# Low-rank tile products of a step in one session, down behind them, and a last step without turns on TensorE

## The reference, cut to what matters

```python
x = x + L0_ffn(L0_cond(x, ..., itok_B_2_6))     # x: (128, 32, 512)
x = x + L1_ffn(L1_cond(x, A, B, itok_B_4_50))

def lora_add(base, inp, A, B):                  # rank 16, matrices picked for each of 128 batches
    t = einsum('bri,bni->bnr', A[ids], inp)
    return base + einsum('bor,bnr->bno', B[ids], t) * 0.5
# L0_cond
gate = lora_add(x @ W_gate.T, x, A_gate, B_gate)            # 512 -> 1376
up   = lora_add(x @ W_up.T,   x, A_up,   B_up)
act  = silu(gate) * up
down = lora_add(act @ W_down.T, act, A_down, B_down)        # 1376 -> 512
# L0_ffn: down @ sign(weight).T + bias
# L1_cond: rank-16 pair picked for each batch (no base product); L1_ffn: linear with 8 adapters, + bias
```

## Time and profile before

| | us |
|---|---|
| median of 3 runs (924.7 to 925.49) | 925.48 |
| the profiled execution | 923.36 |
| its span | 921.4 |
| TensorE busy | 913.8 (99%) |
| DVE busy | 440.0 (48%) |
| ACT busy | 196.0 (21%) |
| POOL busy | 93.4 (10%) |
| granted TensorE clock, mean | 1.00 |

### The profile page before, as it was taken

How to read it: one execution, slowest core, us unless ns; L and a number is a source line. 1 busy time by engine, 2 the same in 40 slices (tenths; PEclk the granted TensorE clock), 3 DMA queues, 4 the chain that set the end, 5 groups by cost and what they waited for, 6 DMA issues and landing times.

```text
span 921.4 us, 27817 instructions
## 1 busy us (share of the span) xinstructions
PE 913.8 (99%) x10528; PEld 709.0 (77%) x10528; DVE 440.0 (48%) x1051; ACT 196.0 (21%) x350; POOL 93.4 (10%) x81
## 2 busy tenths in 40 slices
PE   9999999999999999999999999999999999999998
PEld 6887777778787777777877778787777777877775
DVE  5753435544444454454445544443454454444534
ACT  6742111111212112112111111212112112111111
POOL 0210001111010111101011111010111101011111
PEclk9999999999999999999999999999999999999999
DMA  9934445555454455555445555454455545445541
GB/s 345 414 106 130 120 121 140 141 155 147 134 143 123 132 141 147 155 138 145 130 122 138 141 155 146 134 142 126 127 144 148 153 134 149 124 128 139 141 118 53
DMA packets 148247, 135.22 MB, mean 147 GB/s; under 512 B 53633, under 2 KB 119937, under 8 KB 148097
## 3 DMA queue, kind: packets, MB, share of 16 engines
q1 hardware_dynamic: 90576, 108.16, 40.6%
q10 hardware_dynamic: 56704, 23.62, 10.1%
q0 software_dynamic: 944, 3.15, 0.9%
HBM read 92.11 MB, written 11.01 MB: 112 GB/s over the span
## 4 chain that ended last, share of the span: by engine, by line
PE 99%; DMA 0%; issue 0%; DVE 0%; ACT 0%; SPq 0%
PE gu_ps L790 54%; PE y_ps L834 28%; PE gu_ps L923 4%; PE out_ps L854 3%; PE out_ps L891 3%; PE y_ps L790 1%; PE out_ps L843 1%; PE out_ps L790 1%; PE gu_ps L914 1%; PE out_ps L864 1%; DMA lb_raw<-in_lbw 0%; PE gu_ps L963 0%; PE gu_ps L1035 0%; PE y_ps L895 0%; PE gu_ps L970 0%
## 5 line engine op out<-in xcount | busy, mean ns | idle before, releaser
L834 PE MATMUL y_ps<-down_sb,actT_sb 128*128 128x512 f32 x1056 | 258.9, 398 | 0.0
L790 PE MATMUL gu_ps<-wg_sb,xT_sb 128*128 128x512 f32 (+1 forms) x1152 | 256.0, 371 | 0.0
L790 PE MATMUL gu_ps<-wu_sb,xT_sb 128*128 128x512 f32 (+1 forms) x1152 | 251.4, 367 | 0.0
L790 PEld LDWEIGHTS gu_ps<-wg_sb,xT_sb 128*128 128x128 f32 x1152 | 204.4, 188 | 55.2 <-DVE xT_sb L581 26.1
L834 PEld LDWEIGHTS y_ps<-down_sb,actT_sb 128*128 128x128 f32 x1056 | 191.5, 188 | 68.4 <-DVE actT_sb L581 16.5
L790 PEld LDWEIGHTS gu_ps<-wu_sb,xT_sb 128*128 128x128 f32 x1152 | 206.9, 188 | 29.9
L581 DVE TENSOR_TENSOR actT_sb<-landed,actT_sb 128x512 fp32r<-128x512 f32 (+1 forms) x96 | 76.2, 794 | 113.2 <-ACT actT_sb L426 112.2
L624 DVE STREAM_TRANSPOSE lhs_sb<-t_own 32x32 f32<-32x32 f32 x512 | 103.9, 203 | 7.7
L391 POOL TENSOR_TENSOR x_in<-x_in,bias_sb 128x512 f32<-128x512 f32 x32 | 41.3, 1291 | 581.1 <-DMA x_in<-in_x 581.1
L426 ACT CAST actT_sb<-landed 128x512 fp32r<-128x512 f32 (+1 forms) x96 | 56.1, 584 | 194.0 <-DMA landed<-act_sb 186.8
L601 DVE TENSOR_TENSOR act_sb<-act_sb,gu_ps 128x512 f32<-128x512 f32 (+1 forms) x94 | 58.2, 619 | 70.7 <-ACT act_sb L439 70.7
(11 more groups left out here) (136 smaller groups left out, 450.8 us busy)
## 6 DMA issues: line engine op xcount, KB each, us to landing
b_rows<-in_btab SPq DMA_DIRECT2D x128, 216.0 KB
a_raw<-in_atab SPq DMA_DIRECT2D x128, 152.0 KB, 2.6
xT_raw<-in_xT SPq DMA_DIRECT2D x32, 256.0 KB, 3.6
x_in<-in_x SPq DMA_DIRECT2D x32, 256.0 KB, 3.4
landed<-act_sb ACTq DMA_DIRECT2D x124, 64.0 KB, 2.1
landed<-act_sb SPq DMA_DIRECT2D x124, 64.0 KB, 2.2
x_landed<-x_turn ACTq DMA_DIRECT2D x124, 64.0 KB, 2.2
out_x<-out_sb SPq DMA_DIRECT2D x31, 256.0 KB, 2.5
```

Source lines behind the costliest of these rows:

```text
L790: last = nc.tensor.matmul(o, w, m, start=start and n == 0, stop=stop and n == len(terms) - 1, skip_group_check=not check)
L834: last = nc.tensor.matmul(y_ps[:], actT_sb[:, ACTT_SLOT[c] + n, a, :], down_sb[:, blk, b, :], start=c == begin and n == 0 and (a, b) == (0 ...
```

## The change

On TensorE a step has two sessions in place of three: `small` inside up of chunk 1, and first and second rows back to back behind gate and up of all chunks. The whole of down(g - 1) follows, into a `y_ps` that `down_rows` now begins. Gate 0 waits for `act_done` of all three chunks of the step before. ACT takes the three silus in a row, splits xT in one piece before them, and copies the lhs rows itself (was a DMA). `split_actT` waits for down of the step before, since the activations are split while that runs. SP's order of issue changes.

In the tail the activations of step 31 go the same way as all others, by DMA; x1 of the last step lies in `act_sb[1]`, and the last rank-16 matrices and table rows go to free buffers (`b1_end` in `a_raw`, row group 1 of `cs_rows`). `load_x(31)`, which was the first load of SP's `finish`, comes after these.

```diff
 # SP
             def step(g, prev, pp, nxt):
-                if prev is not None:
-                    send_act(sp, prev, 2)
-                    load_b(g)
-                    load_x(prev)
                 if nxt is not None:
                     load_xT(nxt)
                     load_a(nxt)
                 if prev is not None:
                     load_b1(prev)
+                    load_x(prev)
                 if pp is not None:
                     store(pp)
                 load_sbd(g)
+                send_act(sp, g, 2)
                 if prev is not None:
                     load_c(prev)
+                if nxt is not None:
+                    load_b(nxt)
 
             def finish(g):
-                load_x(g)
-                sp.wait_ge(L["small_mm"], g + 2)
                 for b in range(GB):
                     at = row_of(1, g, b, R1)
-                    sp.dma_start(b1_raw[:, b, :], b1end[bass.ds(at, P), :]).then_inc(L["b1_in"], 16)
-                load_c(g)
+                    sp.dma_start(b1_end[:, b, 0:KC * RANK], b1end[bass.ds(at, P), :]).then_inc(E["b1_in"], 16)
+                load_c(g, 1, E["c_in"])
+                load_x(g)
                 store(g - 1)
 # ACT
             def split_actT(g, c):
                 act.wait_ge(act_in(c), SENT * g + SENT)
+                if not first(g):
+                    act.wait_ge(L["y_mm"], NC * g - NC + c + 1)
...
-                act.dma_start(lhs2_sb[2 * QUAD:P, :], lhs_sb[0:2 * QUAD, :]).then_inc(L["lhs2_in"], 16)
+                copy(lhs2_sb[2 * QUAD:P, :], lhs_sb[0:2 * QUAD, :]).then_inc(L["lhs2_in"], 1)
             def step(g, prev, pp, nxt):
-                if prev is not None:
-                    silu(prev, 1)
-                    silu(prev, 2)
-                    send_act(act, prev, 1)
-                    split_actT(prev, 1)
-                    split_actT(prev, 2)
+                if prev is None:
+                    split_up(2, range(KC))
                 move_ad(g)
                 copy_lhs(g)
-                if prev is None:
-                    split_up(2, range(KC))
-                silu(g, 0)
+                if nxt is not None:
+                    split_xT(nxt)
+                for c in range(NC):
+                    silu(g, c)
                 send_act(act, g, 0)
+                send_act(act, g, 1)
+                split_actT(g, 0)
+                split_actT(g, 1)
                 if prev is not None:
                     send_x1(act, prev)
-                if nxt is not None:
-                    split_xT(nxt)
-                split_actT(g, 0)
+                split_actT(g, 2)
 # DVE: the same order: scale and turn, split_xT(nxt), add_out(pp), gated and turn_act of
 # the three chunks, split_actT(g, 0), add_y(prev), turn_x1(prev), split_actT(g, 1), (g, 2)
             def finish(g):
...
+                dve.wait_ge(L["y_mm"], NC * g + NC)
+                dve.wait_ge(L["x_biased"], g + 1)
+                for half in (slice(0, H // 2), slice(H // 2, H)):
+                    nc.vector.tensor_tensor(x1_end[:, half], x_in[:, half], y_end[:, half], ALU.add).then_inc(E["x1_half"], 1)
                 dve.wait_ge(L["stored"], 16 * (g - 1))
+                add_out(g - 1)
                 dve.wait_ge(E["x1_tr"], 2)
 # TensorE
             def gate(g, c, pieces=range(KC)):
...
+                    pe.wait_ge(L["xT_lo"], g + 1)
+                    after(pe, L["act_done"], g * NC)
...
             def step(g, prev, pp):
+                gate(g, 0)
+                up(g, 0)
+                gate(g, 1)
+                up(g, 1, range(0, 1))
+                small_ready(g, prev, pp)
+                up(g, 1, range(1, 2))
+                small(prev, pp)
+                up(g, 1, range(2, 4))
+                gate(g, 2)
+                up(g, 2, range(0, 3))
+                lora_ready(g, prev, pp)
+                up(g, 2, range(3, 4))
                 first_rows(prev, pp)
+                second_rows()
                 if prev is not None:
+                    for c in range(NC):
+                        down(prev, c).then_inc(L["y_mm"], 1)
...
             def finish(g):
+                for c in range(2):
+                    down(g, c, y_end, begin=True).then_inc(L["y_mm"], 1)
+                pe.wait_ge(L["act_in2"], SENT * (g + 1))
                 pe.wait_ge(L["ad_moved"], g + 1)
+                pe.wait_ge(L["out_done"], g - 1)
+                td_rows().then_inc(L["small_mm"], 1)
+                down(g, 2, y_end, range(0, 2))
                 pe.wait_ge(L["x1T_in"], SENT * g)
                 pe.wait_ge(L["b1_in"], 16 * GB * g)
+                pe.wait_ge(L["small_scaled"], g + 2)
+                t1_rows(b1_raw).then_inc(L["small_mm"], 1)
+                down(g, 2, y_end, range(2, 4))
+                pe.wait_ge(L["lhs_ready"], g + 3)
...
                 for b in range(GB):
+                    last = down_rows(b, y_end, False)
+                last.then_inc(L["y_mm"], 1)
+                for b in range(GB):
+                    last = out_rows(b)
                 last.then_inc(L["first_mm"], 1)
                 keep_busy(2)
```

More of the change, by code:

```diff
@@ L171, in build_adaln_ffn @@
         small_ps = out_ps
+        y_end = gu_ps[2]
         ring_ps = [y_ps, gu_ps[2], gu_ps[3], out_ps]
@@ L207, in hi, with first @@
             return t.bitcast(f32)
+        def first(g):
+            return isinstance(g, int) and g == 0
         def last(g):
@@ L305, in load_b1 @@
             def load_b1(g):
-                if isinstance(g, int) and g == G - 2:
+                if last(g + 1 if isinstance(g, int) else g):
                     sp.wait_ge(L["small_mm"], g + 2)
@@ L429, in split_xT @@
                 act.wait_ge(L["xT_in"], 16 * g + 16)
[L430 to L433, removed]
+                after(act, L["xT_used"], g)
+                copy(xT_sb[:, :, 0, :], xT_raw[:]).then_inc(L["xT_hi"], 1)
             def silu(g, c):
@@ L591, in split_xT @@
             def split_xT(g):
[L592 to L595, removed]
+                dve.wait_ge(L["xT_hi"], g + 1)
+                lo(xT_sb[:, :, 1, :], xT_raw[:], xT_sb[:, :, 0, :]).then_inc(L["xT_lo"], 1)
             def gated(g, c):
@@ L616, in scale_small, with turn_small @@
                                         ).then_inc(L["small_scaled"], 1)
-            def turn_small(g, rows):
+            def turn_small(g, rows, group_of=range(4), signal=L["lhs_ready"]):
                 dve.wait_ge(L["small_scaled"], g + 1)
@@ L691, in finish @@
-                dve.wait_ge(L["x_biased"], g + 1)
-                dve.wait_ge(L["out_done"], g)
-                for half in (slice(0, H // 2), slice(H // 2, H)):
-                    nc.vector.tensor_tensor(x1_sb[:, half], x_in[:, half], y_ps[:, half], ALU.add).then_inc(E["x1_half"], 1)
+                scale_small(g + 1, TD_AT, TD_AT + TD_W)
+                turn_small(g + 1, (3,))
+                scale_small(g + 2, T1_AT, SMALL)
+                turn_small(g + 2, (2,))
+                dve.wait_ge(L["y_mm"], NC * g + NC)
@@ L815, in up @@
                     pe.wait_ge(S["wu_lo"], (c + 1) * KC)
-                if 0 in pieces and c == 1:
-                    after(pe, L["act_done"], g * NC - 1)
                 last = product(gu_ps[GU_BANK[c][1]][:, 0:w], [(xT_sb[:, k, a, :], wu_sb[:, b, k, f:f + w])
@@ L820, in up, with down @@
                                start=0 in pieces, stop=KC - 1 in pieces)
-                if c == NC - 1 and (1 in pieces or KC - 1 in pieces):
+                if c == NC - 1 and KC - 1 in pieces:
                     last.then_inc(L["xT_used"], 1)
-            def down(g, c, blocks=range(4), begin=1):
+            def down(g, c, to=y_ps, blocks=range(4), begin=False):
                 if 0 in blocks:
                     pe.wait_ge(L["actT_lo"], g * NC + c + 1)
-                    if c == begin:
-                        after(pe, L["x1_done"], g)
                 count = len(CHUNK_BLOCKS[c])
@@ L833, in down @@
                     for a, b in THREE:
-                        last = nc.tensor.matmul(y_ps[:], actT_sb[:, ACTT_SLOT[c] + n, a, :], down_sb[:, blk, b, :],
-                                                start=c == begin and n == 0 and (a, b) == (0, 0),
+                        last = nc.tensor.matmul(to[:], actT_sb[:, ACTT_SLOT[c] + n, a, :], down_sb[:, blk, b, :],
+                                                start=begin and (c, n) == (0, 0) and (a, b) == (0, 0),
                                                 stop=c == NC - 1 and n == count - 1 and (a, b) == (1, 0),
@@ L858, in td_rows, with t1_rows @@
                 return last
-            def t1_rows(by_batch=True):
+            def t1_rows(rows, by_batch=True):
                 for k in range(KC):
@@ L902, in first_ready @@
                     pe.wait_ge(L["sbd_in"], 16 * GB * g)
+                    after(pe, L["x1_done"], prev)
                 if pp is not None:
```

173 lines of the change are left out of this document (45 added, 128 removed).

## The result

The changed kernel takes 931.25 us (median, 927.48 to 935.05) against 924.92 (923.46 to 928.11) beside it on the same chip: ratio 1.0066, 95% interval 1.0054 to 1.0079. I had forecast 924.1, no change, within 920.0 to 930.5. The forecast is wrong, in sign and in range.

A forecast was written before the change was run, and what follows sets the result against it. TensorE, at 99% of the chain, was taken to bound the kernel. Loop -10.2, step 0 +2.7 and tail +6.1 sum to -1.4 us: 924.1 against the median 925.48, forecast as no change (chance 0.42), range 920.0 to 930.5.

The forecast's parts named there:

- Part 1: Loop steps 1 to 31, one row session in place of two: saves 0.34 us a step, 10.2 over steps 1 to 30.
- the term for the overlap of the two sets: Merged row session: four passes in a row take 1.97 us instead of 2.13, 0.16 saved a step.
- My lower bound of 0.18: Merged row session: at least 0.18 us saved a step, if the second tiles wait for the whole first set.
- Rival 2: Merged row session: second tiles don't overlap the first, 0.18 us saved a step, +3.4 in all, 928.9; chance 0.12.
- One drain less, at a price between the two bounds: Merged row session, by the skill's tiling-mode rule: one drain saved, worth between 0.18 and 0.40 us a step.
- Part 2: Loop waits the new order creates: gate 0 covered by 4 us, lhs copy by 1.7, x1 by 1.4; back edge 0.
- the back edge: Loop's back edge, now between two dense stretches: cost between 0 and 0.84 us uncovered, taken as 0.
- Rivals 3 and 4: Loop. 3: x1 lands late, 0.5 beyond gives +15, 939, chance 0.05. 4: back edge exposed, 0.15 gives 928.3, chance 0.07.
- Part 3: Step 0, nothing covers the wait at gate 0 of step 1: idle 3.0 us, less 0.3 for the merged session, +2.7.
- Rival 5: Step 0's idling also lowers TensorE's clock: 5 us at half pace, +2.3, 926.4; one in three, within the forecast.
- Part 4: Tail: x_in of step 31 issued at T + 22.7, halves at T + 27.0, TensorE idle about 6 us; +6.1 us net.
- Its clock term: Tail: TensorE's clock falls to half in the 6 us gap, costing 1.4 to 3 us more, taken as 2.0.

The follow-up runs named there:

- experiment 6: Changed kernel with the merge alone undone: down of chunk 0 stands between first and second rows again; 942.24 us, ratio 1.0193.
- after: The changed kernel itself, with the whole change, against the kernel before; 931.25 us, ratio 1.0066.
- after_again: The changed kernel run once more with nothing changed, as control; 929.08 us, ratio 1.0046 to the kernel before.
- x_first: Changed kernel with the load of x_in for the last step moved first in SP's `finish`; 923.99 us, ratio 0.9985.
- keep_busy23: Changed kernel with 23 matmuls nobody reads in place of 2 in the tail's gap; 928.68 us, ratio 1.0038.

## Why the prediction was wrong, point by point

- **Part 1 is the step that failed: the term for the overlap of the two sets.** I wrote "four passes in a row would take 4 x 0.45 + 0.17 = 1.97 us". That reads the array as the only limit. The spacing of the passes was right (466.56 to 467.02, 0.46), but the runs showed that TensorE's intake is a limit too: 30 of the second set's 32 loads come from T + 1.08, when the oldest product is done, and 1.20 from there makes 2.28, longer than the 2.13 of two separate sessions. Enter 0.09 and restart (down in 7.62 where 33 x 0.227 = 7.48: 0.14) make 2.51, against 2.53 before. The 0.18 of borders was earned and spent again. The period, with 0.09 saved, has a bit more than these rows explain; where it comes from stays open. Over steps 1 to 30 it is 30 x 0.09 = 2.7, not 10.2, and that alone turns -1.4 into +6.1. That the medians differ by 6.3 is partly luck: the ledger has 0.9 less in the tail and 1.4 more at the start.
- **My lower bound of 0.18 was not one.** It took a session after a session at the price of two apart. Rival 2 named this failure but gave it 0.18 a step and 928.9; its mechanism (no overlap) happened at a smaller saving still. One drain less, at a price between the two bounds, is not what the runs show.
- **Part 2.** No wait in the loop at gate 0, at x1 or at the lhs copy, as predicted; the back edge cost nothing: at the loop's head, 476.46, TensorE has no idle time and gate 0 runs at pace. Rivals 3 and 4 didn't occur. Rival 3's mechanism is real, however: experiment 6 spent the slack and paid 0.24 a step.
- **Part 3 was right**: +2.7 and +2.7. Rival 5 comes and goes: the clock held in the profiles of after and after_again and fell in those of x_first, keep_busy23, the four with other tile orders and both with two sessions, with the same 2.82 us of idling, for 1.4 to 1.6 us over gate 0 and up 0 (2.3 predicted).
- **Part 4 was right in what bound the tail**: x_in's issue at T + 22.7 and the halves at T + 26.9 as worked out, +5.2 for +6.1. Its clock term was too large, 1.1 and not 2.0; the 0.45 us a matmul that it was priced by comes from the first 5 us of the kernel, where the view of the stretches shows 1.00 for the granted clock, so that those rows don't show the level. And it left a wait out: the activations of step 31 now go by DMA, and TensorE waits 1.11 us for them before down(31) (the row at 902.71). y was ready at T + 21.6 and not at T + 20.4; x_in, later still, hid that.
- Left over: 0.65 us in step 2, where TensorE's last small tiles pause for issue, 1.55 against 0.90 before, and the 1.4 us at the start, which is scatter.

## What to carry to other kernels

Merging two sessions of small tiles saves their borders only if the engine can take in the second set while the first runs: count the instructions of a set (here 16 two-pass products fill the intake) before pricing an overlap by array places. When an order is moved, look at what lands last in the first and the last step, where no neighbour covers it: one load at the end of a queue cost 5 us and one wait on three chunks instead of one cost 2.7, more than the merge earned in 28 iterations. And slack of some 1 us on a side chain is a resource of the whole order: when ACT's silus came 2.3 us later, it was gone, at 0.24 us a step.

## What the runs showed of the hardware that I had not expected

- TensorE stops taking the weight loads of two-pass 32x32 products behind the 16th product (32 loads), but for one or two that go with a place of their own, and takes the bulk only when the oldest product's second pass ends, whatever places in the array are free. In step 0, where the first set has 8 products (16 loads), 13 of the second set's loads go out by 73.36, while the first set still runs, and the other 19 wait behind a pause:

```profile
73.00 0.36 PEld L894 LDWEIGHTS gu_ps<-b_rows,lhs_sb 32*32 32x32 f32 x11
73.53 0.42 PEld L894 LDWEIGHTS gu_ps<-b_rows,lhs_sb 32*32 32x32 f32 x19 [0.17 <-issue]
```

The session starts at 72.91 there. By T + 0.13 there are loads for four of the eight second-set products whose places nobody uses in step 0, those among the first 16 products of the session; the other four, with places as free, get none until T + 0.8. So the limit is a count. Whether it counts products, matmuls or all instructions isn't shown, since every product here has two passes.

- A border between row tiles and dense matmuls costs 0.09 us to enter and 0.09 to 0.14 to leave, merged or not.
- The same 2.82 us of idle TensorE left the granted clock at 1.00 in two profiles and was followed by 0.50 in eight; the idle 4.5 to 5.8 us in the tail brought it down in all eight profiles that had them.
